# An attention and mixture-of-experts kernel: the low parts of seven batches' context made on GpSimd instead of VectorE

## The chip, the cores and the metric

The kernel runs on one core of one Trainium2 chip. The metric is the device time of the whole program in microseconds (us), as the median of three runs. The engines are TensorE (PE in the profile, with its weight loads as PEld), VectorE (DVE), ScalarE (ACT), GpSimd (POOL) and SyncE (SP), which in this kernel only issues DMAs.

## The reference

Eight batches of 512 tokens with 512 columns go through cross attention against a context of the same shape, and then through a mixture of eight experts, of which each token takes two:

```
x = x + xattn(layernorm(x), ctx, ctx, Wq, bq, Wk, bk, Wv, bv, Wo, bo)   # 16 heads of 32
x = x + ffn(layernorm(x), router, gate_up, down)                       # top 2 of 8 experts

K = ctx @ Wk.T + bk ;  V = ctx @ Wv.T + bv ;  Q = ln(x) @ Wq.T + bq
attn = softmax(Q K^T / sqrt(32)) ;  out = (attn V) @ Wo.T + bo
```

All arrays are 32 bit floats.

## The kernel before

There are three stages one after the other: attention for all batches (to about 950 us of the profile), a short routing stage, and the expert stage (39 tiles of 256 tokens). The change lies in the attention stage alone.

**Units and steps.** The attention works on 32 units. Unit u is batch b = u // 4 and a group c = u % 4 of four heads (128 columns). Step s scores and weighs unit s and meanwhile projects K, Q and V of unit s + 2. A step has eight rounds. In each round TensorE makes one pair of score tiles for the row maximum of unit s + 1 ("max", line 542), which VectorE reduces (line 802) before the next pair may be written. It also makes two score tiles of unit s (line 554), of which ScalarE takes the exponential (line 671). GpSimd adds the exponentials up into `acc` (lines 980 and 983), two heads at a time, six additions of 128x1024 to a unit. TensorE sums `acc` over the partitions (line 574) in round 3 of the next step, and the first addition of the next unit waits for that.

**Split operands.** The context is multiplied in three passes of a fast 32 bit format (`fp32r`): high by high, high by low and low by high. For this ScalarE makes the high part of the transposed context (line 637, `ctx_hi`), and the low part is the raw context less the high part (line 776, `ctx_lo`): for each batch four instructions of 128x512, one for each chunk k of 128 context columns. `ctx_raw` and `ctxT_lo` are the same memory. TensorE waits for chunk k's low part before the matmuls of that chunk (line 496), in the K projection of the first unit of a batch.

**The order of the work.** It is written out by the function `step(s)` as a list of keys by rounds. Each engine walks the same list and emits what is its own, so that an engine's program order is the order of the list, and an instruction that waits holds up all that stand behind it on its engine. The part of `step` that places the context of the next batch is the branch for c = 2:

```
elif c == 2:
    at(0, ("q", u, 0), ("ctx_hi", b + 1, 0), ("ctx_hi", b + 1, 1))
    at(1, ("q", u, 1), ("ctx_hi", b + 1, 2), ("ctx_hi", b + 1, 3), ("ctx_lo", b + 1, 0), ("ctx_lo", b + 1, 1))
    at(2, ("ctx_lo", b + 1, 2), ("ctx_lo", b + 1, 3))
    at(3, ("low", u, "q"), ("k", u, 0))
    at(4, ("k", u, 1))
```

So steps 2, 6, 10, 14, 18, 22 and 26 hold the four `ctx_lo` of one batch each, in rounds 1 and 2, and TensorE uses them in rounds 3 (chunks 0 and 1) and 4 (chunks 2 and 3). The first batch is dealt with ahead of the steps.

**What else GpSimd does in such a step**: the last addition of the unit before in round 1, two small instructions for a layer norm (lines 965 and 967), one addition of 128x512 in round 2 (line 972, the output bias), from step 11 on two indirect DMAs of the token list in round 3 (line 43), and then the additions of the step's own unit from round 4 on.

**What SP does in such a step**: it issues the DMAs that copy q and k, high and low, to the places from which the score matmuls read them (line 626), 24 issues for one unit, with loads of x (line 1062) and stores between them. The maxima of the next step's first round wait for the last of these, `ks<-k_lo`.

Of the kernel before, what the change touches and what calls it, by code (L numbers as in the profile page):

```python
# [5 lines left out]
ALU = mybir.AluOpType  # L6
ACT = mybir.ActivationFunctionType
AX = mybir.AxisListType
F32 = mybir.dt.float32
# [59 lines left out]
def attention_stage(nc, x, ctx_t, w_t, bq, bk, bv, bo, router_wt, router_b, out, xln_dram, w_rows, w_stored, token_list, listed, stored, route, ident):  # L69
# [17 lines left out]
    with ExitStack() as ctx:  # L87
# [539 lines left out]
                            source[HD * r:HD * (r + 1), :].bitcast(F32)).then_inc(landed, 16)  # L627


        def on_act(e):  # L630
            def weight_hi(n, k):
                e.wait_ge(w_in[n], 16)
# [94 lines left out]
        def on_dve(e):  # L727
# [41 lines left out]
            def weight_lo(n, k):  # L769
                e.wait_ge(w_hi_made[n].sem, w_hi_made[n][k])  # L770
                e.tensor_tensor(w[n][1][:, k, :], w_raw[n][:, k, :], w[n][0][:, k, :].bitcast(F32),
                                ALU.subtract).then_inc(w_lo_made[n].sem, 1)

            def ctx_lo(b, k):
                e.wait_ge(ctx_hi_made.sem, ctx_hi_made[b, k])
                e.tensor_tensor(ctxT[1][:, k, :], ctx_raw[:, k, :], ctxT[0][:, k, :].bitcast(F32),
                                ALU.subtract).then_inc(ctx_lo_made.sem, 1)

            def add_router_bias(n):
                e.wait_ge(logits_summed.sem, logits_summed[n])  # L780
# [129 lines left out]
            for kind, *what in ORDER:  # L910
# [12 lines left out]
                elif kind == "norm":  # L923
                    normalise(*what)
                elif kind == "x2":
                    add_residual(*what)
                elif kind == "ln2":
                    ln2(*what)
                elif kind == "turn_x" and what[0] == 0:
                    first_x_copy(what[1])  # L930
                elif kind == "stats":
                    ln1_stats(*what)
                elif kind == "mean":
                    ln1_mean(*what)
                elif kind == "shift":
                    ln1_shift(*what)
                elif kind == "split":
                    weight_lo(*what)
                elif kind == "ctx_lo":
                    ctx_lo(*what)  # L940
                elif kind == "logit_out":
                    add_router_bias(*what)
                elif kind == "best":
                    if what == [0, 0]:
                        route_consts()
                    best_experts(*what)
                elif kind == "count":
                    count_experts(*what)
                elif kind == "share":
                    share(*what)  # L950
                elif kind == "place":
                    place_tokens(*what)


        def on_pool(e):
# [48 lines left out]
            for kind, *what in ORDER:  # L1004
# [5 lines left out]
                    stack(e, "q", 0, LOW_AT["q"], lo["q"], first_lo["q"])  # L1010
                elif kind == "mean" and what[0]:
                    ln1_rstd(*what)
                elif kind == "add":
                    add_weights(*what)
                elif kind == "rstd":
# [886 lines left out]
```

## Time and profile before

| | before |
|---|---|
| median of three runs | 1720.36 us |
| the three runs | 1716.99, 1720.36, 1723.82 us |
| profiled execution, its own time | 1732.28 us |
| its span | 1730.5 us |
| attention from the first to the last maxima turned (46.8 to 926.8 us) | 880 us, 27.5 us a step |
| busy over the span: PE, DVE, ACT, POOL | 92%, 74%, 38%, 48% |

The profile is one execution, which took 12 us more than the median of the runs. A row of the timeline gives the start, the duration, the engine, the line, the operation with its output and input tiles, the count, and in brackets how long the engine sat idle before it and which instruction ended that. Rows with a count above 1 are instructions that ran back to back and are shown as one. Two neighbouring matmuls overlap, so their durations add up to more than the time they take.

### The profile page before, as it was taken

Reading aid. Unit: us, or ns where it says so; the run is one execution under the profiler, and the core shown is the slowest. Engines: PE = TensorE matmul, PEld = TensorE weight load, DVE = VectorE, ACT = ScalarE, POOL = GpSimd, SP = SyncE. Lnnn points to the kernel's source line nnn. Section 1 sums busy time; section 2 is a strip of 40 time slices with the busy share of each in tenths; the row PEclk is TensorE's granted clock in tenths of the full one; section 3 lists DMA queues with packets and bytes.
Section 4 is the critical chain, followed back from the end, with each engine's and each line's share of the span. In section 5 each row is a group of like instructions: output and inputs, shape, how many; then the busy total and the mean of one; then the engine's idle time right before and its main releaser. Section 6 shows DMA issues by size and latency. Waiting matters only on the chain. (4 is left out here: it accounts for less than half of the span.)

```text
span 1730.5 us, 30244 instructions
## 1 busy us (share of the span) xinstructions
PE 1597.8 (92%) x9612; PEld 1168.4 (68%) x9612; DVE 1272.5 (74%) x2414; ACT 658.1 (38%) x1267; POOL 837.5 (48%) x634
## 2 busy tenths in 40 slices
PE   6889999999899999999998469999999999999995
PEld 4445555555555555555553259999999998999994
DVE  5575777878668778687685668778888778777873
ACT  3354544535445445354444133223323234222320
POOL 3364656566566676566678321423333333423232
PEclk9999999999999999999999769999999999999997
DMA  6342333443434433424331161324543253324321
GB/s 221 84 121 66 106 112 85 112 104 88 121 80 111 103 94 94 116 75 110 92 99 33 56 223 50 101 85 166 172 147 123 87 204 121 107 85 149 116 86 61
DMA packets 101125, 188.99 MB, mean 109 GB/s; under 512 B 28192, under 2 KB 29600, under 8 KB 100960
## 3 DMA queue, kind: packets, MB, share of 16 engines
q1 hardware_dynamic: 79936, 124.25, 25.4%
q0 software_dynamic: 20832, 62.49, 11.4%
q8 instruction: 77, 1.26, 0.4%
q14 instruction: 88, 0.72, 0.2%
q10 hardware_dynamic: 192, 0.26, 0.0%
HBM read 204.32 MB, written 37.51 MB: 140 GB/s over the span
## 5 line engine op out<-in xcount | busy, mean ns | idle before, releaser
L802 DVE TENSOR_REDUCE negmax<-max_ps 128x2 f32<-128x1024 f32 x252 | 307.4, 1220 | 175.5 <-PE max_ps L542 174.1
L671 ACT ACTIVATE pt<-work 128x512 f32<-128x512 f32 x512 | 278.6, 595 | 263.5 <-PE work L554 256.7
L983 POOL TENSOR_TENSOR acc<-acc,pt 128x1024 f32<-128x1024 f32 x128 | 303.8, 2377 | 134.1 <-ACT pt L671 134.1
L1486 PE MATMUL gu_ps<-xgT_hi,wg_hi 128*128 128x256 f32 x1248 | 349.3, 280 | 2.3 <-DVE xgT_lo L1601 1.5
L1486 PE MATMUL gu_ps<-xgT_lo,wg_hi 128*128 128x256 f32 x1248 | 345.8, 277 | 0.0
L1486 PE MATMUL gu_ps<-xgT_hi,wg_lo 128*128 128x256 f32 x1248 | 345.5, 277 | 0.0
L980 POOL TENSOR_TENSOR acc<-pt 128x1024 f32<-128x1024 f32 x64 | 153.3, 2396 | 200.2 <-PE work L574 132.0
L1486 PEld LDWEIGHTS gu_ps<-xgT_hi,wg_hi 128*128 128x128 f32 x1248 | 235.2, 188 | 3.0 <-issue 1.9
L1747 POOL DMA_INDIRECT out<-acc,token_of x78 | 77.2, 989 | 330.4 <-DVE acc L1645 324.6
L1486 PEld LDWEIGHTS gu_ps<-xgT_lo,wg_hi 128*128 128x128 f32 x1248 | 235.5, 189 | 0.1
L1486 PEld LDWEIGHTS gu_ps<-xgT_hi,wg_lo 128*128 128x128 f32 x1248 | 235.2, 188 | 0.0
L542 PE MATMUL max_ps<-ks,qs 96*128 96x512 f32 x504 | 196.9, 472 | 29.7 <-DVE negmax L802 12.1
L1556 ACT ACTIVATE sig<-gate 128x256 f32<-128x256 f32 x156 | 65.4, 419 | 323.0 <-DVE gate L1609 321.4
L554 PE MATMUL work<-qs,ks 98*128 98x512 f32 x512 | 170.7, 411 | 12.2 <-DMA qs<-m_lo 6.6
L542 PEld LDWEIGHTS max_ps<-ks,qs 96*128 96x128 f32 x504 | 88.0, 194 | 89.8 <-issue 63.0
L566 PE MATMUL o_ps<-pt,v 128*32 128x512 f32 x1024 | 137.2, 608 | 1.6 <-ACT pt L671 1.1
L1500 PE MATMUL d_ps<-wd_hi,hid_hi 128*128 128x512 f32 x312 | 125.3, 401 | 13.7 <-DVE acc L1642 13.3
L554 PEld LDWEIGHTS work<-qs,ks 98*128 98x128 f32 x512 | 97.6, 193 | 48.9 <-issue 13.4
L1742 POOL DMA_INDIRECT acc<-out,token_of x78 | 80.7, 1035 | 101.0 <-DMA out<-acc,token_of 88.6
L504 PE MATMUL work<-xT,wq 128*128 128x512 f32 x256 | 124.0, 607 | 1.8 <-DMA wq<-wq_t 1.8
L1500 PE MATMUL d_ps<-wd_lo,hid_hi 128*128 128x512 f32 x312 | 125.0, 401 | 0.0
L1500 PE MATMUL d_ps<-wd_hi,hid_lo 128*128 128x512 f32 x312 | 124.3, 398 | 0.0
(221 smaller groups left out, 2902.2 us busy)
## 6 DMA issues: line engine op xcount, KB each, us to landing
raw_g<-w_gate_up SPq DMA_DIRECT2D x39, 2048.0 KB
raw_d<-w_down SPq DMA_DIRECT2D x39, 1024.0 KB
qs<-q_hi SPq DMA_DIRECT2D x252, 64.0 KB
ks<-k_hi SPq DMA_DIRECT2D x252, 64.0 KB
bd<-b_down SPq DMA_DIRECT2D x39, 256.0 KB
x_in<-x SPq DMA_DIRECT2D x36, 256.0 KB, 3.3
ctxT_raw<-ctx_t SPq DMA_DIRECT2D x32, 256.0 KB, 4.1
xln_dram<-x SPq DMA_DIRECT2D x32, 256.0 KB, 2.8
```

The lines of the kernel that those rows point to most:

```text
L504: ins = e.matmul(to[:, :], wq[:, k, cols], xT[:, k, :], start=(k == 0), stop=(k == C - 1))
L542: ins = e.matmul(pair_of(u, r)[:, j, :], qs[i][0:3 * HD, h, t * P:(t + 1) * P], ks[i][0:3 * HD, h, :], start=True, stop=True)
L554: e.matmul(to[:, :], ks[i][0:3 * HD + 2, h, k * P:(k + 1) * P], qs[i][0:3 * HD + 2, h, :], start=True, stop=True).then_inc(exp_ready.sem, 1)
L566: ins = e.matmul(o_ps[u % 2][HD * h:HD * (h + 1), :], v[:, k, c * P + HD * h:c * P + HD * (h + 1)], pt[k % 2][:, h, :], start=(k == 0), st ...
L671: e.activation(pt[k % 2][:, h, :], in_work("exp", u, k, h)[:, :], ACT.Exp, scale=scale).then_inc(exped.sem, 1)
L802: e.tensor_reduce(negmax[:, u % 2, n:n + 2], pair_of(u, r)[:, :, :], AX.X, ALU.max, negate=True).then_inc(maxed.sem, 1)
L980: e.tensor_tensor(acc[:, heads, :], pt[0][:, heads, :], pt[1][:, heads, :], ALU.add).then_inc(added.sem, 1)
L983: e.tensor_tensor(acc[:, heads, :], acc[:, heads, :], pt[k % 2][:, heads, :], ALU.add).then_inc(added.sem, 1)
L1486: ins = e.matmul(gu_ps[n % GU_BANKS][:, part, :], wg[s][pw][:, k, cols], xgT[s][px][:, k, :], start=(k == 0 and m == 0), stop=(k == KD - 1 ...
L1500: ins = e.matmul(d_ps[j][:, :], hid[s][px][:, k, j * P:(j + 1) * P], wd[s][pw][:, k, :], start=(k == 0 and m == 0), stop=(k == KF - 1 and ...
L1742: e.indirect_dma_start(out=acc[s][:, j, :], out_offset=None, in_=out_rows, in_offset=slot_rows(i, j)).then_inc(acc_in[s], 16)
L1747: e.indirect_dma_start(out=out_rows, out_offset=slot_rows(i, j), in_=acc[i % 2][:, j, :], in_offset=None).then_inc(scattered.sem, 16)
```

## The change

The helper that makes one low part moves out of VectorE's program and takes the engine as an argument. VectorE calls it for batch 0, GpSimd for all other batches. The waits, the semaphores, the operands and the place in the list of keys are the same.

```diff
+        def ctx_lo(e, b, k):
+            e.wait_ge(ctx_hi_made.sem, ctx_hi_made[b, k])
+            e.tensor_tensor(ctxT[1][:, k, :], ctx_raw[:, k, :], ctxT[0][:, k, :].bitcast(F32),
+                            ALU.subtract).then_inc(ctx_lo_made.sem, 1)
...
-            def ctx_lo(b, k):
-                e.wait_ge(ctx_hi_made.sem, ctx_hi_made[b, k])
-                e.tensor_tensor(ctxT[1][:, k, :], ctx_raw[:, k, :], ctxT[0][:, k, :].bitcast(F32),
-                                ALU.subtract).then_inc(ctx_lo_made.sem, 1)
...
-                elif kind == "ctx_lo":
-                    ctx_lo(*what)
+                elif kind == "ctx_lo" and what[0] == 0:
+                    ctx_lo(e, *what)
...
+                elif kind == "ctx_lo" and what[0]:
+                    ctx_lo(e, *what)
```

GpSimd's program in step 14, from the layer norm's small instructions to the unit's additions. `rstd` is the layer norm's factor, `x<-x,bo_rows` the output bias, `token_list` the indirect DMAs. Before:

```order
L965 TENSOR_TENSOR var_eps<-mv,eps_col 128x1
L967 TENSOR_TENSOR rstd<-var_eps,minus_half 128x1
L972 TENSOR_TENSOR x<-x,bo_rows 128x512
L43 DMA token_list<-consts,pos 32768x1 x2
L980 TENSOR_TENSOR acc<-pt 128x1024 x2
L983 TENSOR_TENSOR acc<-acc,pt 128x1024 x4
```

The same place in the changed kernel (line 776 is line 632 there):

```order
L965 TENSOR_TENSOR var_eps<-mv,eps_col 128x1
L967 TENSOR_TENSOR rstd<-var_eps,minus_half 128x1
L632 TENSOR_TENSOR ctxT_lo<-ctxT_raw,ctxT_hi 128x512 x2
L972 TENSOR_TENSOR x<-x,bo_rows 128x512
L632 TENSOR_TENSOR ctxT_lo<-ctxT_raw,ctxT_hi 128x512 x2
L43 DMA token_list<-consts,pos 32768x1 x2
L980 TENSOR_TENSOR acc<-pt 128x1024 x2
```

Two low parts stand ahead of the bias addition now and two behind it, and the DMAs and the unit's additions come after them.

VectorE's program in the same step, from the maxima of round 1 to the low part of q in round 3. `negmax` are the maxima, lines 899 to 908 the places of the tokens. Before:

```order
L802 TENSOR_REDUCE negmax<-max_ps 128x2
L781 TENSOR_TENSOR logits<-work,rb_rows 128x8
L776 TENSOR_TENSOR ctxT_lo<-ctxT_raw,ctxT_hi 128x512 x2
L802 TENSOR_REDUCE negmax<-max_ps 128x2
L776 TENSOR_TENSOR ctxT_lo<-ctxT_raw,ctxT_hi 128x512 x2
L802 TENSOR_REDUCE negmax<-max_ps 128x2
L899 TENSOR_TENSOR ranks<-work,consts 128x32
```

In the changed kernel:

```order
L802 TENSOR_REDUCE negmax<-max_ps 128x2
L781 TENSOR_TENSOR logits<-work,rb_rows 128x8
L802 TENSOR_REDUCE negmax<-max_ps 128x2 x2
L899 TENSOR_TENSOR ranks<-work,consts 128x32
```

The four low parts are gone from between the reductions, and nothing else on VectorE has moved. The orders of PE, ACT and SP are the same in both kernels.

## Rows read from the trace of the kernel before

**Rows 1.** The page, span and busy time of each engine.
```profile
span 1730.5 us, 30244 instructions
...
PE 1597.8 (92%) x9612; PEld 1168.4 (68%) x9612; DVE 1272.5 (74%) x2414; ACT 658.1 (38%) x1267; POOL 837.5 (48%) x634
```

**Rows 2.** Busy time in the attention's 32 steps: PE, PEld, DVE, ACT, POOL, clock, DMA.
```profile
46.80:926.80 880.00, 834.57 (x4268) 482.71 (x4269) 651.95 (x1021) 408.22 (x757) 546.45 (x322) 0.98 0.37 97
```

**Rows 3.** Groups by form, 100 to 1000 us: busy us, mean ns | idle before.
```profile
L972 POOL TENSOR_TENSOR x<-x,bo_rows 128x512 f32<-128x512 f32 x28 | 35.8, 1279 | 0.0
...
L776 DVE TENSOR_TENSOR ctxT_lo<-ctxT_raw,ctxT_hi 128x512 fp32r<-128x512 f32 x28 | 25.6, 955 | 0.0
...
L868 DVE TENSOR_TENSOR expo<-logits,best 128x32 f32<-128x32 f32 x6 | 12.0, 1998 | 0.0
```

**Rows 4.** Line 776 alone: shortest, median and longest ns.
```profile
L776 DVE TENSOR_TENSOR ctxT_lo<-ctxT_raw,ctxT_hi x32: 677/684/1806, 16.6 to 803.8; 128x512 fp32r<-128x512 f32 x32
```

**Rows 5.** The longest waits of PE in 46.8 to 926.8: total us, times, longest.
```profile
PE max_ps L542 <- DVE negmax L802: 12.1, 18, 0.9
PE max_ps L542 <- issue: 8.6, 3, 4.2
...
PE max_ps L542 <- DMA ks<-k_lo: 3.5, 1, 3.5
```

**Rows 6.** Timeline of PE in step 14 (440.8 to 469.2) and after.
```profile
450.09 0.74 PE L542 MATMUL max_ps<-ks,qs 96*128 96x512 f32 x2 [0.79 <-DVE negmax L802]
...
453.38 0.50 PE L496 MATMUL work<-ctxT_hi,wk_hi 128*128 128x512 f32 x1
...
455.81 0.40 PE L496 MATMUL work<-ctxT_hi,wk_hi 128*128 128x512 f32 x1
...
456.50 0.39 PE L496 MATMUL work<-ctxT_hi,wk_hi 128*128 128x512 f32 x1
...
473.66 1.19 PE L542 MATMUL max_ps<-ks,qs 96*128 96x512 f32 x2 [4.20 <-issue]
```

**Rows 7.** Timeline of VectorE in step 14.
```profile
446.17 2.39 DVE L776 TENSOR_TENSOR ctxT_lo<-ctxT_raw,ctxT_hi 128x512 fp32r<-128x512 f32 x2
448.81 1.22 DVE L802 TENSOR_REDUCE negmax<-max_ps 128x2 f32<-128x1024 f32 x1 [0.25 <-PE max_ps L542]
449.95 1.28 DVE L776 TENSOR_TENSOR ctxT_lo<-ctxT_raw,ctxT_hi 128x512 fp32r<-128x512 f32 x2
451.15 1.22 DVE L802 TENSOR_REDUCE negmax<-max_ps 128x2 f32<-128x1024 f32 x1
...
455.54 1.23 DVE L802 TENSOR_REDUCE negmax<-max_ps 128x2 f32<-128x1024 f32 x1 [1.30 <-PE max_ps L542]
```

**Rows 8.** Timeline of GpSimd in step 14.
```profile
446.16 1.25 POOL L972 TENSOR_TENSOR x<-x,bo_rows 128x512 f32<-128x512 f32 x1
...
449.17 0.97 POOL L43 DMA_INDIRECT token_list<-consts,pos  x1 [0.30 <-issue]
453.63 2.40 POOL L980 TENSOR_TENSOR acc<-pt 128x1024 f32<-128x1024 f32 x1 [3.49 <-PE work L574]
456.94 2.54 POOL L980 TENSOR_TENSOR acc<-pt 128x1024 f32<-128x1024 f32 x1 [0.91 <-ACT pt L671]
...
463.15 2.38 POOL L983 TENSOR_TENSOR acc<-acc,pt 128x1024 f32<-128x1024 f32 x1 [1.33 <-ACT pt L671]
```

**Rows 9.** Timeline of ScalarE in step 14.
```profile
448.93 1.14 ACT L637 ACTIVATE ctxT_hi<-ctxT_raw 128x512 fp32r<-128x512 f32 x2
...
461.99 1.09 ACT L671 ACTIVATE pt<-work 128x512 f32<-128x512 f32 x2 [1.48 <-PE work L554]
```

**Rows 10.** Timeline of SP's DMA issues in steps 14 and 18.
```profile
449.06 9.77 SPq L626 DMA_DIRECT2D qs<-q_hi  x8
...
469.60 2.41 SPq L626 DMA_DIRECT2D ks<-k_lo  x4
...
585.44 2.41 SPq L626 DMA_DIRECT2D ks<-k_lo  x4
```

## The prediction

> **What bounds the kernel now.** I read the page first, then the busy time of the attention stage, the waits of TensorE in it, and last the timelines of all five engines in one of the seven steps that the change touches. The page shows TensorE busy for 92% of the span, VectorE for 74%, GpSimd for 48% [rows 1]. In the 880 us of the attention steps TensorE is busy for 834.6 us, which leaves 45 us; VectorE is busy for 652 us, GpSimd for 546 us [rows 2]. So TensorE sets the pace, and work taken from VectorE pays only where TensorE waits for VectorE. The largest such wait is the one of the score matmuls for the row maxima, 12.1 us in 18 waits of at most 0.9 us; the other large ones wait for the copies of k and q: 3.5 us for `ks<-k_lo`, and 8.6 us in three waits for which the view names nothing ("issue") [rows 5].
>
> I take step 14 as the pattern, since the seven steps (2, 6, 10, 14, 18, 22, 26) repeat each other to a few tenths of a us around the low parts. Steps 2, 6 and 10 have no token list DMAs on GpSimd, which makes them easier, not harder.
>
> **What VectorE gives up.** Seven batches by four instructions are 28, with 955 ns in the mean, 25.6 us busy in all [rows 3]. The bare duration is the median of 684 ns; the longest is 1806 ns [rows 4]. The long one is the first of each first pair: in step 14 the pair begins at 446.17 and takes 2.39 us, while GpSimd adds the bias from 446.16 to 447.41; the second pair, with GpSimd on its DMAs, takes 1.28 us [rows 7, 8]. So a low part on VectorE now waits out an addition on GpSimd, and after the change there is nothing left to wait.
>
> How much of the 25.6 us does TensorE feel? I follow the reductions, since the score matmuls wait for these.
> - The first pair ends at 448.56. The next reduction starts at 448.81, after VectorE sat idle for 0.25 us until TensorE's scores were there [rows 7]. The pair delays nothing.
> - That reduction ends at 450.03, and the next scores start at 450.09 after a wait of 0.79 us [rows 6, 7]. This wait looks like VectorE's fault, but its reduction started as early as its scores allowed. It is the length of one reduction with too little other work for TensorE beside it, and stays.
> - The second pair ends at 451.23, so the reduction at 451.15 starts right behind it. The scores that it reads began at 450.09 and took 0.74 us, ended at 450.83, so it could start about 0.3 us sooner. The next scores were only written between the two halves of the K projection, between 453.38 and 455.81, and the reduction had ended at 452.37. There were over 2 us to spare.
> - The next reduction, at 455.54, has VectorE idle for 1.30 us ahead of it, ended by TensorE [rows 7]. There VectorE is back in step, and nothing earlier reaches past it.
>
> The gain is 0 us in each of the seven steps. The bound on the side of a gain is the whole wait of 0.79 us by seven, 5.5 us. I take 0, because the reduction ahead of the wait was itself waiting for TensorE.
>
> **What GpSimd takes on.** The trace has no subtraction to `fp32r` on GpSimd. The nearest row is the addition of the same 128x512 with two inputs, 1.28 us [rows 3]. The same elements on VectorE take 0.68 us [rows 4], the lower bound; the upper one is GpSimd's 128x1024 addition with 2.38 us [rows 8]. I take 1.28, since it has the same engine, inputs and size. 28 by 1.28 is 36 us of GpSimd, which sits idle for 334 of the 880 us [rows 2].
>
> In step 14 this comes to: GpSimd is free at 446.16. The high parts of chunks 0 and 1 were made in round 0. Low parts 0 and 1 to 448.72; the bias addition to 449.97; the high parts of chunks 2 and 3 are ready by 450.07 [rows 9]; low parts 2 and 3 to 452.6. TensorE's K projection starts at 453.38 with chunk 0, and comes to chunk 2 at 455.81 and to chunk 3 at 456.50 [rows 6]. The margins are 4.7 us for the first chunk, over 4 for chunk 2 and 3.9 for chunk 3. TensorE waits for nothing: 0 us.
>
> Queued behind them are the two token list DMAs. They now take from the end of the bias addition, 447.41, to 450.14, which is 2.73 us [rows 8], and would end at 455.3. The unit's first addition started at 453.63, after GpSimd had been idle for 3.49 us until TensorE's sums were made, so it moves back by 1.7 us, to end at 457.7. Who waits for it is the exponential of the unit's third tile, at 461.99 [rows 9]: 4.3 us of margin. The second addition starts at 457.7 instead of 456.94 and the third about 0.7 us late, and the 1.33 us of idle time ahead of the addition at 463.15 take up the rest [rows 8]. In steps 2, 6 and 10, without the DMAs, the low parts end before the first addition can start. Again 0 us.
>
> At the upper bound of 2.38 us the four would end at 448.54, 450.92, then the bias at 452.2, and 454.6 and 456.9. Chunk 3 would come 0.4 us late for 456.50, and the first addition at 462.1 would be 0.1 us late for the exponential. That is 0.5 us in a step, some 4 us in all. With the lower bound nothing changes.
>
> The row for VectorE's small operation of line 868, 128x32 in 1998 ns [rows 3], shows again that a VectorE instruction with two inputs in SBUF can wait for a whole GpSimd addition. In step 14 the token places have two such instructions (line 903), which would now start near 452.2, while the last low part runs to 452.6: 0.4 us, at most 1.28 us, against the 1.30 us of idle time that VectorE has ahead of 455.54. The cost is 0 us.
>
> The Trainium skill, in "SBUF — State Buffer", on the ports, says that GpSimd and a VectorE instruction with two inputs in SBUF share one pair of ports under an exclusive lock, so that the later one blocks for the whole of the other. The 1806 ns against 684 agree with that. By it the change takes a lock user away from VectorE and gives GpSimd a longer hold, which here would meet only line 903. The page "GPSIMD Engine Reference", section on performance against the Vector engine, speaks against the change: elementwise work with two inputs belongs on VectorE, being some two times slower on GpSimd. The trace agrees on the ratio (1279 ns to 684). If the low parts lay on the path that sets the end, that would cost 28 by 0.6 us, 17 us and not 0; by the margins above they do not.
>
> **The sum.** 0 from VectorE, 0 from GpSimd, against the profiled execution's own 1732.3 us (span 1730.5), so 1732.3. The median of the runs was 12 us below this profile, 1720.4, and I carry the difference of 0 over to it: 1720.4 us.
>
> **The rivals.**
> - Faster, by VectorE's relief. If the reduction behind the 0.79 us waits were in truth held back by the low parts, seven of these would go: 5.5 us, 1715. For more, the waits for `ks<-k_lo` and "issue" would have to go as well, 3.5 and 8.6 us [rows 5]; all of it gives 17.6 us, 1703. Against it stands that SP issues `ks<-k_lo` only at 469.60, long after VectorE made it, because SP is late with its own queue: eight issues of `qs<-q_hi` took it 9.77 us from 449.06 [rows 10]. TensorE's wait of 4.20 us to 473.66 is this wait [rows 6]. VectorE has no part in it.
> - Slower, by SP's queue. In these steps SP has little to spare: in step 18 its last `ks<-k_lo` was issued by 587.85 [rows 10], and the next scores come at about 589.5. The token list DMAs of GpSimd move from 447.6 to about 452.7, into the same time as SP's issues of q and k. If the two kinds of DMA held each other up, every one of the steps 14, 18, 22 and 26 would show the longest wait, 4.2 us, where the three "issue" waits together are 8.6 us now, 1.3 of it in a step without these DMAs. So 16.8 less 7.3 is 9.5 us, 1730. It decides from the point at which SP is 2 us later than in step 18. For it speaks that a pause of SP costs TensorE at once; against it that SP pauses in steps with and without DMAs of GpSimd beside it.
> - Slower, by a GpSimd that is slow with `fp32r`: the 4 us of the upper bound, 1724. It hardly leaves the band of no change.
>
> **How the numbers follow.** A measurement can tell about 0.5%, 8.6 us, from no change. I give the forecast of no change 0.77, GpSimd's slowness another 0.05 inside the same band, relief of VectorE 0.08 and SP's queue 0.10. Relief has its small form of 5.5 us inside the band and its large form outside; of the 0.08 I put 0.02 inside. SP's queue has 0.01 inside. So faster 0.06, same 0.85, slower 0.09. The range starts from the runs' own spread of 3.4 us to each side, and takes in the gain of 5.5 us below and the 4 us above with a part of SP's case: 1713 to 1728.
>
> **What would show it right or wrong.** Right: on GpSimd 28 rows of line 632 of about 1.28 us; VectorE's busy time lower by some 26 us, GpSimd's higher by 36; the 0.79 us wait ahead of the scores in each of the seven steps still there; no wait of the K projection for GpSimd; the unit's first addition 1.7 us later in step 14 with no exponential waiting for it. Wrong: a row of line 496 that waits for `ctxT_lo`, low parts much over 1.3 us, exponentials that wait for GpSimd, the 0.79 us waits gone, or waits for `ks<-k_lo` longer or more frequent in the step behind each step with c = 2.

## The result and the profile after

| | before | after |
|---|---|---|
| median of the runs made side by side | 1722.09 us (1716.99 to 1723.84, 4 runs) | 1739.62 us (1734.64 to 1741.89, 4 runs) |
| profiled execution, its own time | 1732.28 us | 1740.52 us |
| its span | 1730.5 us | 1738.8 us |
| attention, first to last maxima turned | 879.9 us | 887.8 us |

The change makes the kernel slower: after to before is 1.0103, 95% interval 1.007 to 1.0135, some 17.5 us. A second measurement of the same kernel gave 1.0111 (1.0088 to 1.0134). The forecast was no change, 1720.4 us, with a range of 1713 to 1728 us.

The page of the kernel after, span and busy time, as in [rows 1]:

```profile
span 1738.8 us, 30244 instructions
...
PE 1598.9 (92%) x9612; PEld 1168.4 (67%) x9612; DVE 1265.2 (73%) x2386; ACT 656.4 (38%) x1267; POOL 867.7 (50%) x662
```

The line view of the new low part in the kernel after (shortest, median and longest ns; first and last start):

```profile
L632 POOL TENSOR_TENSOR ctxT_lo<-ctxT_raw,ctxT_hi x28: 1251/1269/1285, 107.9 to 807.4; 128x512 fp32r<-128x512 f32 x28
L632 DVE TENSOR_TENSOR ctxT_lo<-ctxT_raw,ctxT_hi x4: 681/681/683, 16.9 to 20.5; 128x512 fp32r<-128x512 f32 x4
```

So the 28 low parts cost GpSimd 1.27 us each, as forecast; its busy time rose by 30.2 us. But VectorE, which lost 28 instructions of 25.6 us [rows 3], is only 7.3 us less busy. Some instructions on VectorE must have grown instead. The one that matters is found in the waits of TensorE from the first to the last step of the kernel after (total us, times, longest), which is [rows 5] again:

```profile
PE max_ps L542 <- DVE negmax L802: 12.7, 20, 0.8
PE work L459 <- DVE x L771: 9.2, 3, 3.1
...
PE max_ps L542 <- issue: 4.0, 3, 2.1
...
PE max_ps L542 <- DMA ks<-k_lo: 3.1, 1, 3.1
```

The second line is new: in the kernel before, line 459 waits for no layer norm. Line 459 turns the layer norm's result over, and line 771 (766 in the kernel before) makes it: `x = (x - mean) * rstd`, one input tile in SBUF and two factors a row. Its line view, after and then before:

```profile
L771 DVE TENSOR_SCALAR x<-x,mv,rstd x28: 536/538/5524, 196.3 to 966.4; 128x512 f32<-128x512 f32 x28
```

```profile
L766 DVE TENSOR_SCALAR x<-x,mv,rstd x28: 536/539/1496, 194.7 to 958.8; 128x512 f32<-128x512 f32 x28
```

The median is the same, the longest went from 1.5 to 5.5 us. Three instructions take 5.5 us, one in each of the steps 18, 22 and 26. GpSimd in step 18 of the kernel after:

```profile
566.90 2.49 POOL L632 TENSOR_TENSOR ctxT_lo<-ctxT_raw,ctxT_hi 128x512 fp32r<-128x512 f32 x2
569.35 1.27 POOL L972 TENSOR_TENSOR x<-x,bo_rows 128x512 f32<-128x512 f32 x1
570.59 2.51 POOL L632 TENSOR_TENSOR ctxT_lo<-ctxT_raw,ctxT_hi 128x512 fp32r<-128x512 f32 x2
573.27 1.04 POOL L43 DMA_INDIRECT token_list<-consts,pos  x1 [0.18 <-issue]
574.62 0.96 POOL L43 DMA_INDIRECT token_list<-consts,pos  x1 [0.30 <-issue]
575.61 4.74 POOL L980 TENSOR_TENSOR acc<-pt 128x1024 f32<-128x1024 f32 x2
580.32 2.33 POOL L983 TENSOR_TENSOR acc<-acc,pt 128x1024 f32<-128x1024 f32 x1
```

VectorE in the same stretch:

```profile
573.86 0.43 DVE L908 CAST pos<-pos_f 128x8 int32<-128x8 f32 x1
...
576.27 1.23 DVE L802 TENSOR_REDUCE negmax<-max_ps 128x2 f32<-128x1024 f32 x1 [1.58 <-PE max_ps L542]
577.41 5.52 DVE L771 TENSOR_SCALAR x<-x,mv,rstd 128x512 f32<-128x512 f32 x1
582.86 0.94 DVE L819 RECIPROCAL inv<-inv 128x128 f32<-128x128 f32 x1
```

And VectorE and GpSimd at that place in the kernel before:

```profile
576.70 0.54 DVE L766 TENSOR_SCALAR x<-x,mv,rstd 128x512 f32<-128x512 f32 x1
```

```profile
573.64 2.41 POOL L980 TENSOR_TENSOR acc<-pt 128x1024 f32<-128x1024 f32 x1 [3.49 <-PE work L574]
576.96 2.52 POOL L980 TENSOR_TENSOR acc<-pt 128x1024 f32<-128x1024 f32 x1 [0.91 <-ACT pt L671]
```

Read with the step's start (561.56 after, 560.84 before), the layer norm comes 15.86 us into the step in both kernels. Before, the first addition ran from 12.80 to 15.20 and the second from 16.12: the layer norm started in the gap of 0.9 us between them, and it was the second addition that took 2.52 us instead of 2.4. After, the first addition starts at 14.05, since the two list DMAs end only then. It now ends later than the second could have started, so the first three additions run without a gap, from 575.61 to 582.65, and the layer norm is done at 582.93. It waited not for the one addition that ran when it came, but for the whole row of three.

Not every instruction of VectorE waits so. The reciprocal of line 819 reads and writes SBUF alone, too, and 38 of its 124 instances began while a GpSimd operation of over 1 us was running, but none took longer than 0.95 us:

```profile
L819 DVE RECIPROCAL inv<-inv x124: 939/942/952, 93.0 to 950.0; 128x128 f32<-128x128 f32 x124
```

TensorE in the kernel after, step 18:

```profile
578.95 1.06 PE L566 MATMUL o_ps<-pt,v 128*32 128x512 f32 x8
583.08 1.08 PE L459 MATMUL work<-ident,x 128*128 128x128 f32 x4 [3.07 <-DVE x L771]
583.82 0.56 PE L518 MATMUL work<-wv_hi,ctxT_hi 128*128 128x256 f32 x1
584.18 0.41 PE L518 MATMUL work<-wv_lo,ctxT_hi 128*128 128x256 f32 x1
...
586.19 0.28 PE L518 MATMUL work<-wv_hi,ctxT_lo 128*128 128x256 f32 x1
```

Busy time by stretches of that step in the kernel after (PE, PEld, DVE, ACT, POOL, granted clock, DMA share, GB/s):

```profile
566.00:582.00 16.00, 13.22 (x67) 6.64 (x66) 10.87 (x13) 8.27 (x15) 15.41 (x13) 1.00 0.53 59
583.00:586.00 3.00, 2.92 (x14) 2.95 (x15) 2.90 (x4) 0.60 (x1) 0.00 (x0) 0.50 0.59 146
586.00:592.00 6.00, 6.00 (x36) 3.85 (x35) 4.59 (x8) 1.69 (x4) 2.38 (x1) 1.00 0.81 232
```

TensorE stood for 3.07 us, and then the granted clock was 0.50 (1.2 GHz) for the next 3 us, in which the matmuls of line 518 start 0.21 us apart instead of 0.115. The step takes 32.99 us instead of 28.38; 3.07 of the 4.6 us are the pause, and the lower clock makes up the rest. Three such steps are 13.8 us.

Step 14 of the same profile escaped. Its first two additions and its layer norm:

```profile
458.50 4.96 POOL L980 TENSOR_TENSOR acc<-pt 128x1024 f32<-128x1024 f32 x2
```

```profile
460.57 0.64 DVE L771 TENSOR_SCALAR x<-x,mv,rstd 128x512 f32<-128x512 f32 x1
```

Here the layer norm came 0.3 us later, 16.14 us into the step, and so did the exponentials that the second addition reads: they were ready 0.16 us before the first addition ended, against 0.45 us in step 18. The pair takes 4.96 us instead of 4.74, and the layer norm got in between the two. Which of the two delays let it in is not shown.

### The profile page after: what moved, and what is told of

Same layout as the page of the kernel before. It is cut to its first block and busy times, and to the rows that moved or that the text cites. A ratio compares the mean times of both kernels' runs of the same rounds, so it can differ in the third digit from the quotient of the medians.

```text
span 1738.8 us, 30244 instructions
## 1 busy us (share of the span) xinstructions
PE 1598.9 (92%) x9612; PEld 1168.4 (67%) x9612; DVE 1265.2 (73%) x2386; ACT 656.4 (38%) x1267; POOL 867.7 (50%) x662
## 3 DMA queue, kind: packets, MB, share of 16 engines
q0 software_dynamic: 20832, 62.49, 11.1%
## 5 line engine op out<-in xcount | busy, mean ns | idle before, releaser
L542 PE MATMUL max_ps<-ks,qs 96*128 96x512 f32 x504 | 195.8, 470 | 26.4 <-DVE negmax L802 12.7
L554 PE MATMUL work<-qs,ks 98*128 98x512 f32 x512 | 169.6, 409 | 11.6 <-DMA qs<-m_lo 6.7
L1502 PE MATMUL d_ps<-wd_hi,hid_hi 128*128 128x512 f32 x312 | 125.7, 403 | 14.5 <-DVE acc L1644 13.2
```

The lines of the kernel that those rows point to most:

```text
L542: ins = e.matmul(pair_of(u, r)[:, j, :], qs[i][0:3 * HD, h, t * P:(t + 1) * P], ks[i][0:3 * HD, h, :], start=True, stop=True)
L554: e.matmul(to[:, :], ks[i][0:3 * HD + 2, h, k * P:(k + 1) * P], qs[i][0:3 * HD + 2, h, :], start=True, stop=True).then_inc(exp_ready.sem, 1)
L1502: ins = e.matmul(d_ps[j][:, :], hid[s][px][:, k, j * P:(j + 1) * P], wd[s][pw][:, k, :], start=(k == 0 and m == 0), stop=(k == KF - 1 and ...
```

## The experiments

**The theories.** A: the first addition comes so late that GpSimd's gap closes, and the layer norm of line 771 waits inside its own duration until GpSimd pauses. The main rival, D in most of the expectations: the token list DMAs of GpSimd, moved to a later time, meet SP's copies of q and k, and the next step's scores wait for these. Further rivals say in the expectations themselves what they are.

I cut each profile into steps by the starts of line 548, and count for the last four steps with c = 2 (14, 18, 22, 26) what they take over 28.36 us each, and for the steps behind them (c = 3: 15, 19, 23, 27) what they take over 26.97. In the latter the excess is mostly TensorE waiting for the copies of k and q, and its lower clock behind such a wait; in the three versions with the lists moved out of the c = 2 steps it is something else, as told below for lists_out_after. A ratio is taken against runs of the kernel before on the same chip, whose medians were 1722.1 to 1725.4 us, so times of different versions compare best by their ratios.

| kernel | ratio to before (95%) | c = 2 steps over, us | c = 3 steps over, us |
|---|---|---|---|
| before | 1 | 1.2 | 13.3 |
| after | 1.0103 (1.007, 1.0135) | 14.2 | 4.3 |
| after_again | 1.0111 (1.0088, 1.0134) | 15.7 | 7.1 |
| first_three | 1.0005 (0.9985, 1.0025) | 0.3 | 7.2 |
| last_four | 1.0079 (1.0054, 1.0104) | 19.7 | 0.1 |
| ln2_accum | 1.0048 (1.003, 1.0067) | 0.2 | 7.6 |
| dummy_pool | 1.0110 (1.0071, 1.0149) | 25.8 | 0.0 |
| half | 1.0017 (1.0001, 1.0032) | 0.2 | 12.7 |
| lists_later | 1.0136 (1.0109, 1.0162) | 1.3 | 23.6 |
| ln2_sooner | 1.0089 (1.0062, 1.0116) | 0.1 | 20.0 |
| lists_out_after | 1.0021 (1.0, 1.0042) | 0.4 | 12.4 |
| lists_out_before | 1.0027 (1.001, 1.0045) | 0.6 | 11.4 |
| x_later | 0.9955 (0.9934, 0.9975) | 0.4 | 8.0 |
| both | 0.9998 (0.9979, 1.0017) | 1.4 | 11.1 |
| filler2 | 1.0045 (1.0024, 1.0065) | 13.5 | 1.1 |
| filler4 | 1.0054 (1.003, 1.0077) | 16.6 | 3.5 |
| bias_later | 1.0040 (1.0023, 1.0057) | 11.6 | 0.3 |
| x_later_lists | 0.9994 (0.9972, 1.0016) | 9.8 | 0.0 |

The two columns are of one execution each, the ratio of several. The profile of before is an unlucky one: its own time is 10 us over the 1722.09 us, and its c = 3 column is higher than that of first_three, which is as fast as before.

**The changed kernel again.** after_again is the changed kernel with no edit, for its time beside other runs.

> The changed kernel once more, for a second profile of it. Theory A: 1739 to 1740; each of the steps 14, 18, 22 and 26 either takes 28.4 to 28.7 us or some 33.0, according to whether line 771 got in between the two additions, with at least three of the four at 33.0.

It gave 1742.57 us and the same picture: line 771 with 5.50 to 5.52 us in steps 18, 22 and 26, 0.66 in step 14.

**Which batches.** first_three moves only the low parts of batches 1 to 3 to GpSimd (steps 2, 6 and 10, which hold no list DMAs), last_four only those of batches 4 to 7 (steps 14 to 26).

```diff
-                elif kind == "ctx_lo" and what[0]:
+                elif kind == "ctx_lo" and 0 < what[0] < 4:     # first_three
+                elif kind == "ctx_lo" and what[0] > 3:         # last_four
```

VectorE makes the others.

> The low parts of batches 1 to 3 on GpSimd (steps 2, 6, 10), all others on VectorE as before. Theory A, the port: in the changed kernel the list DMAs and the unit's first two additions on GpSimd move back by some 1.5 us, GpSimd then runs additions back to back, and VectorE's layer norm instruction (line 771, 5.5 us instead of 0.54 in steps 18, 22 and 26) waits for them. In steps 2, 6 and 10 there are no list DMAs, the first addition isn't late, so the time is that of before, 1722 (within 2 us), and line 771 never takes over 1.5 us. Theory B, a cost in proportion to the low parts moved: 3/7 of 17.5 us, 1729.6.

> The low parts of batches 4 to 7 on GpSimd (steps 14, 18, 22, 26), all others on VectorE. Theory A: the whole loss, 1739 to 1740, with three or four of these steps 4.6 us longer (28.4 to 33.0). Theory B: 4/7 of 17.5 us, 1732.1.

first_three took 1722.58 us, as expected. last_four took 1735.46 us, which is some 13.6 us by the ratio and a little less than the whole loss. Line 771 in the profile of last_four:

```profile
L771 DVE TENSOR_SCALAR x<-x,mv,rstd x28: 536/540/5495, 195.8 to 964.2; 128x512 f32<-128x512 f32 x28
```

The cost lies in the steps that hold the list DMAs. In last_four all four of them have the long layer norm (5.47 to 5.50 us).

**Taking the stall away at its own instruction.** ln2_accum is the changed kernel with one more output for line 771, a sum over the row. Its `x` is then not the layer norm's, so the text reads only its times.

```diff
-                                ALU.subtract, ALU.mult).then_inc(ln2_made.sem, 1)
+                                ALU.subtract, ALU.mult, accum_out=unused[:, :]).then_inc(ln2_made.sem, 1)
```

> The changed kernel, with VectorE's layer norm instruction (tensor_scalar, 128x512 from SBUF to SBUF) in the form that also writes an accumulator to a tile that nobody reads. The Trainium skill, SBUF - State Buffer, section Who interferes with whom, has this form leave GpSimd's ports alone. Theory A with that rule: the instruction takes longer on its own (some 0.7 us instead of 0.54, the 128x512 rows of one element a cycle) but never 5.5 us, no transposition (line 459) waits 3 us for it, and the time is near that of before: 1722 to 1725. If what it waits for isn't the ports, it still takes 5.5 us in three or four steps and the time is 1740.

Line 772 (771 in the changed kernel) in its profile:

```profile
L772 DVE TENSOR_SCALAR_CACHE_REDUCE x<-x,mv,rstd x28: 795/797/805, 198.9 to 958.2; 128x512 f32<-128x512 f32 x28
```

It takes 0.80 us instead of 0.54, but never more than 0.81, though GpSimd's first additions are as late and as close as in the changed kernel (14.03 us into step 18, 4.77 us for two). So the instruction did as expected, and the c = 2 steps have no excess. The time did not: 1730.06 us is over the 1722 to 1725 expected. The stall is gone and some 9 of the 17.5 us with it; 8.2 us stay (5 to 11.5 by the interval), which the stall does not explain. They can't be laid on the low parts either. Beside first_three, the profile of ln2_accum is 9.9 us longer, 1.3 us of it between the first and last maxima turned and 7.6 us in the stages behind the attention, which the change does not touch and which here work on other values. That part of the span lies between 796.9 and 804.5 us in all profiles, 803.8 in that of before.

**Making the stall without the change.** dummy_pool is the kernel before, with one extra GpSimd operation of 128x512 wherever the change puts a low part on GpSimd.

```diff
+                elif kind == "ctx_lo" and what[0]:
+                    extra()      # bo_rows = bo_rows * 1, on GpSimd
```

> The kernel before, where VectorE makes all low parts, with four additional instructions of 128x512 on GpSimd at the places where the changed kernel has its low parts (the bias row times one, in place, which changes no value). Theory A: GpSimd's later additions are the cause, whoever makes the low parts, so the time is that of the changed kernel or more, about 1740, with line 766 at 3 to 5.5 us in steps 14, 18, 22 and 26. Theory C, the loss comes from what VectorE no longer does or from TensorE's wait for GpSimd's low parts: 1722.

TensorE's waits in its profile from 440 us on:

```profile
PE work L459 <- DVE x L766: 16.2, 4, 4.1
```

It took 1742.45 us, as expected. Line 766 takes 6.5 us in all four steps and TensorE stands for 4.04. So who makes the low parts does not matter to the stall; that GpSimd is late does.

**Half of the change.** half moves only chunks 0 and 1 to GpSimd, which fits into its idle time ahead of the first addition.

```diff
-                elif kind == "ctx_lo" and what[0]:
+                elif kind == "ctx_lo" and what[0] and what[1] < 2:
```

> The changed kernel with only chunks 0 and 1 of batches 1 to 7 on GpSimd, chunks 2 and 3 back on VectorE. Theory A: GpSimd is free some 2.5 us sooner, before the sums are made, so the first addition isn't late, and all 17.5 us come back: 1722. Theory B, in proportion: half the loss, 1731.

(The low parts of each engine have a semaphore of their own here.) The first addition is back at 12.8 to 13.0, line 771 at 0.54 us in these steps, and the time, 1727.57 us, within 0.2% of before.

**Making room by moving the list DMAs or the layer norm.** lists_later issues the list DMAs of the c = 2 steps in round 7; ln2_sooner makes the layer norm a round earlier, with the store of its result, which SP issues.

```diff
-                at(3, ("list", g, t))
+                at(7 if c == 2 else 3, ("list", g, t))                            # lists_later
-                at(2 if s == B * C else 4 if c == 2 else 3, ("ln2", s - 5))
+                at(2 if s == B * C else 3, ("ln2", s - 5))                        # ln2_sooner
```

> The changed kernel, with GpSimd's two token list DMAs of each step with c = 2 moved from round 3 to round 7, behind the unit's third addition. All 28 low parts stay on GpSimd. Theory A, the port: the unit's first two additions are on time again (first at 12.8 us into the step, second at 16.1, a gap between them), line 771 takes 0.54 us, the steps with c = 2 take 28.4 us and not 33.0, and the time is that of before: 1722. Theory B, that low parts on GpSimd cost by themselves: 1739.

> The changed kernel, with the layer norm of the steps with c = 2 (line 771 on VectorE, and its store on SP) in round 3, as in the other steps, instead of round 4. GpSimd's program and its late additions are as in the changed kernel. Theory A: line 771 then stands beside the last low part or the list DMAs of GpSimd, waits at most 1.3 us for one instruction, and no transposition waits for it; the steps 18, 22 and 26 take 28.4 us and not 33.0, the time is 1722 to 1727. If late additions cost by another way (ScalarE, the sums), it stays at 1740.

Both removed the stall (line 771 at 0.54 and at most 0.63 us in the c = 2 steps, which take what they took before), and both missed the 1722 to 1727 us expected, with 1745.72 and 1741.74: they lost more in the c = 3 steps, 23.6 and 20.0 us, than the stall costs. TensorE's waits from 440 us on, first of lists_later, then ln2_sooner, then the kernel before:

```profile
PE max_ps L542 <- issue: 15.5, 3, 7.3
```

```profile
PE max_ps L542 <- issue: 12.5, 3, 6.7
```

```profile
PE max_ps L542 <- issue: 7.3, 2, 4.2
```

These are the first scores of a c = 3 step, which wait for `ks<-k_lo`. Where TensorE waits for it in a step without list DMAs, they come 1.6 us after SP's last issue of it. In lists_later it was 7.9, 8.6 and 3.7 us, in ln2_sooner up to 8.1 us: the issue is on time and the data is late. In other steps SP itself pauses, as in [rows 10]. So the place of the list DMAs among SP's copies seems to have a price of its own. It is not the place alone: ln2_sooner has the lists where the changed kernel has them, and there the same scores come 3.9 us (5.5 in after_again) after the last issue in step 15. Below the stall the lateness is hidden: a TensorE that is 4.6 us late for another reason does not wait for these copies, which is why the c = 3 column of last_four and dummy_pool is nearly 0.

**The list DMAs out of these steps.** lists_out_after and lists_out_before move them into the next step, for the changed kernel and the kernel before alike.

```diff
-            if g in groups[:-3]:
+            if g in groups[:-3] and (c != 2 or s + 2 not in units):
+            if c == 3 and s - 15 in range(0, 16, T):
+                at(3, ("list", (s - 15) // T, 3))
```

> The changed kernel, with the two token list DMAs of the steps 14, 18, 22 and 26 moved to round 3 of the step behind each, which has no low parts (steps 15, 19, 23 and 27 then have four). Theory A, the port, says that the loss goes: line 771 at 0.54 us in all steps, steps with c = 2 at 28.4 us. And theory D, formed from the traces so far, says that GpSimd's token list DMAs slow the DMA queues: where they stand at 7 to 9 us into a step, SP's eight issues of q's high part took 7.4 to 9.8 us in most of the steps 14, 22 and 26 instead of 5.0; where they stood at 25 to 28 us, k's low part landed up to 8.6 us after its last issue instead of 1.6, and TensorE waited up to 7.3 us. With them out of these steps, D expects waits of at most 1 us at the start of the steps 15, 19, 23 and 27, so 1716 to 1719, under the kernel before. Without D: 1722 to 1725.

> The same move of the token list DMAs in the kernel before, with all low parts on VectorE. Theory D: the same time as lists_out_after, 1716 to 1719, since without the collision it is of no account which engine makes the low parts. If GpSimd's low parts cost or gain something by themselves, the two differ by over 3 us.

This is the plainest comparison of the two engines: with nothing that makes GpSimd late, the low parts on GpSimd give 1730.46 us and on VectorE 1729.53. The difference of 0.9 us for 28 instructions is within the noise, the 0 of the forecast. The 1716 to 1719 us expected for both failed to come. Their c = 3 steps are as long as before for another reason: in step 15 of lists_out_after TensorE waits 3.55 us for ScalarE's copy of the turned layer norm, in step 19 2.77 us for a reduction. That the four list DMAs in these steps are behind these waits is likely and not shown.

**SP's queue.** x_later is the kernel before with three of the four loads of x behind the copies of k and q; both joins it with lists_out_before.

```diff
-                for t in range(T):
-                    at(1 + t, ("load_x", b + 2, t))
+                at(1, ("load_x", b + 2, 0))
+                at(6, ("load_x", b + 2, 1))
...
+                at(0, ("load_x", b + 2, 2))
+                at(1, ("load_x", b + 2, 3))
```

> The kernel before, with three of the four loads of x that SP issues among the copies of q and k in a step with c = 2 moved behind them (round 6, and rounds 0 and 1 of the next step). Theory A says that TensorE's waits of 1.3 to 4.2 us at the start of the steps with c = 3 are SP's lateness alone: SP's last issue of k's low part then comes 1.7 us sooner, and up to 1.7 us of each such wait goes, some 4 to 6 us in all: 1717. If SP's lateness were made up of something else (its pauses between issues), no change: 1722.

> The kernel before with both moves: the loads of x behind the copies of q and k (x_later), and the token list DMAs of the steps with c = 2 in the step behind (lists_out_before). x_later alone was 6 us under the kernel before, lists_out_before is expected some 4 us under it, mostly from the same waits: 1713 to 1717, the fastest of all. If the two save the same waits, no better than x_later, 1718.

In five of the seven steps behind one with c = 2 SP issues the last `ks<-k_lo` 1.0 to 1.7 us sooner than in the profile of before, and x_later takes 1718.71 us (1717 was expected), by the ratio 7.7 us less than before and the fastest of all. Joined with the moved lists the gain is gone, against the 1713 to 1717 us expected.

**The stall with no DMA moved.** filler2 and filler4 are the kernel before with 2 or 4 extra GpSimd operations in the steps 14, 18, 22 and 26, behind the list DMAs.

```diff
+                    if t == 3 and g < 4:
+                        for _ in range(2):     # filler4: 4
+                            extra()
```

> The kernel before (low parts on VectorE) with 2 extra GpSimd operations of one 128x512 bias row times one in steps 14, 18, 22 and 26, behind the list DMAs and ahead of the unit's first addition; no DMA is moved. Theory A (the first addition must not come so late that it runs into the next one while the layer norm's tensor_scalar stands between them): GpSimd is through with the extra work at about 12.3 us into the step, the first addition still starts at 12.8, line 766 stays at 0.54 us, steps at 28.4, time 1722 to 1725. Rival B (any GpSimd work added in these steps costs, by its port or by its heat): about 4 us, a quarter of the changed kernel's loss or more, 1727 or above.

> The same with 4 such operations: GpSimd is through at about 15.3 us, so that the first addition starts 2.5 us late and joins the second; still no DMA is moved. Theory A: line 766 takes 5.5 us or more in all four steps, TensorE stands 3 to 4 us ahead of the transposes, steps of 33 to 35 us, 1738 to 1746. Rival C (the changed kernel's loss is that of the later list DMAs): steps keep 28.4 to 29, time below 1728.

Theory A's numbers missed both. filler2 should have been free and cost 1.0045, the time that rival B had; filler4 should have cost 1738 to 1746 and took 1734.64, more than rival C allowed. GpSimd in step 18 of filler2 (it starts at 559.04):

```profile
568.37 2.51 POOL L980 TENSOR_TENSOR bo_rows<-bo_rows,ones 128x512 f32<-128x512 f32 x2
571.86 2.39 POOL L990 TENSOR_TENSOR acc<-pt 128x1024 f32<-128x1024 f32 x1 [0.98 <-PE work L574]
576.45 2.38 POOL L990 TENSOR_TENSOR acc<-pt 128x1024 f32<-128x1024 f32 x1 [2.19 <-ACT pt L671]
579.19 2.38 POOL L993 TENSOR_TENSOR acc<-acc,pt 128x1024 f32<-128x1024 f32 x1 [0.35 <-ACT pt L671]
```

VectorE beside it:

```profile
568.17 3.26 DVE L776 TENSOR_TENSOR ctxT_lo<-ctxT_raw,ctxT_hi 128x512 fp32r<-128x512 f32 x2
571.35 1.21 DVE L802 TENSOR_REDUCE negmax<-max_ps 128x2 f32<-128x1024 f32 x1
...
572.70 1.83 DVE L903 TENSOR_TENSOR hot<-hot,ranks 128x32 f32<-128x32 f32 x2
...
576.88 2.24 DVE L766 TENSOR_SCALAR x<-x,mv,rstd 128x512 f32<-128x512 f32 x1
```

The first addition is on time, as expected. But the two fillers hold up VectorE's second low part (3.26 us for the pair instead of 1.28), the reduction and the token places behind it come 2 us late, and so they run into the first addition, which they had passed by a hair: in the kernel before the last of them, line 908, was done at 12.7 us into the step and the addition started at 12.8. They wait until it ends at 574.25, TensorE's next tile waits 1.28 us for line 908, and the step takes 31.73 us. The stall is the same, at another instruction.

That wait also makes the second addition late, and the layer norm, coming at 576.88, meets it: it takes 2.24 us. It is done 0.29 us after the addition's end at 578.83, in the gap of 0.35 us in which GpSimd waits for an exponential before its third addition. No transposition waits for it, but VectorE is late behind it, and TensorE later waits 0.72 us for the low part of k. So a gap of 0.35 us is enough to let VectorE in. In filler4 the additions begin at 14.5, 1.7 us late and not the 2.5 expected, and the conversion of line 908 waits for the first one: TensorE stands for 2.0 to 2.1 us in three of the steps and for 1.3 in the fourth, the layer norm takes 2.2 us, and the steps take 32.5 us.

**Both causes undone at once.** bias_later is the changed kernel with the list DMAs ahead of the low parts and the bias addition moved to round 6.

```diff
-                at(2, ("bo", s - 2))
+                at(6 if c == 2 and s + 2 in units else 2, ("bo", s - 2))
-                at(3, ("list", g, t))
+                at(1 if c == 2 and s + 2 in units else 3, ("list", g, t))
```

> The changed kernel, all 28 units with the low parts on GpSimd, but in the steps with c = 2 the list DMAs are issued in round 1 ahead of the low parts and the bias addition (line 972) moves to round 6, into GpSimd's gap. Theory A+D (port stall, and list DMAs not later than before): the first addition at 13.0 us or sooner, line 771 at 0.54 us, steps 28.4, no late k copies, 1722 within 3. Rival: the low parts cost something by themselves on GpSimd (slower by more than 4 us with both undone). If the bias addition in the gap pushes the first addition behind 13.5 us, the stall is back and the time is near 1740.

It missed too: 1731.25 us, 1.0040, over the 1722 within 3 us that were expected. In step 18 the first addition is at 12.80 and the c = 3 steps are clean (0.3 us over), but GpSimd in step 18 (from 557.13) reads:

```profile
564.98 4.98 POOL L632 TENSOR_TENSOR ctxT_lo<-ctxT_raw,ctxT_hi 128x512 fp32r<-128x512 f32 x4
569.93 2.39 POOL L980 TENSOR_TENSOR acc<-pt 128x1024 f32<-128x1024 f32 x1
```

And VectorE:

```profile
568.31 0.18 DVE L899 TENSOR_TENSOR ranks<-work,consts 128x32 f32<-128x32 f32 x1
568.52 3.85 DVE L903 TENSOR_TENSOR hot<-hot,ranks 128x32 f32<-128x32 f32 x2
```

Two instructions of 128x32, 0.42 us elsewhere, take 3.85 us: the first came at 568.52, while the low parts ran until 569.96, and the second was let in at the end of the addition, 572.32. There was no gap between the low parts and the addition. In steps 14 and 22 it is the conversion of line 908 that waits for the addition, and in all four the layer norm takes 2.2 us, as in filler2. The steps take 31.0 to 31.5 us.

**The lists sooner in the fastest version.**

```diff
-                at(3, ("list", g, t))
+                at(1 if c == 2 and s + 2 in units else 3, ("list", g, t))   # on x_later
```

> The kernel before with three of the four x loads moved behind the k and q copies (as x_later, 0.9955) and the list DMAs of the steps with c = 2 in round 1, ahead of the bias addition. Theory D: the lists are served before SP issues the next unit's copies, SP's pauses shrink, and it is 0.994 to 0.9955 of before. If the lists in round 1 meet other copies, 0.9955 to 1.0.

The c = 3 steps have no excess left at all, which shows what the place of the list DMAs is worth. But the bias addition behind them runs into VectorE's low parts, and line 910 (908 in the others) comes just too late for the gap:

```profile
565.92 2.38 DVE L910 CAST pos<-pos_f 128x8 int32<-128x8 f32 x1
```

The first addition began at 565.88. A conversion of eight columns, 0.17 us in x_later, waits for it, the layer norm behind it takes 2.2 us, and the c = 2 steps take 30.8 us. What the one side gave, the other took: 0.9994, where 0.994 to 0.9955 was expected.

## Why the prediction was wrong

**The step that failed** is the sentence "Again 0 us" on what is queued behind the low parts. I asked who waits for the additions of GpSimd, found the exponential with 4.3 us of margin, and stopped. The right question is also who runs beside them. With a first addition 1.7 us later I had it end at 457.7 and the second start there: my own numbers said that the gap between the two closes. I did not look at what stood in it, line 766 on VectorE.

**The lock was named and given to the wrong instruction.** The prediction drew on the Trainium skill, "SBUF — State Buffer", for instructions with two inputs in SBUF, and checked line 903. The Trainium skill, same page, section "Who interferes with whom", also lists the plain scalar operation (except in the form that writes an accumulator) and the cast among the ones that can take the shared ports. The trace agrees: 5.52 us for line 771 and 2.38 us for the cast of line 910 beside an addition, and never over 0.81 us in the accumulator form.

**And its price was taken too low.** I put the most that one collision can cost at 1.28 us, one GpSimd instruction. The Trainium skill, in the same section, says that whoever issues first has the shared ports for the whole instruction and the other blocks. The trace shows more than that: VectorE waited for all that GpSimd ran without a gap, three additions in step 18 (until 582.65, having come at 577.41), low parts and an addition in bias_later. A gap of 0.35 us was enough in filler2.

**The smaller terms.** VectorE's gain of 0 was right: the wait of 0.79 us ahead of the scores (0.85 in steps 2 and 6, as before) is there in all seven steps of the kernel after. The low part's 1.28 us was right (1.27). TensorE waits for no low part. The first addition came 1.25 us late instead of 1.7.

**The rival of SP's queue** was priced at 9.5 us. In the kernel after it is not seen at that price: its c = 3 steps lost 4.3 us (7.1 in after_again), where before lost 13.3 and first_three, as fast as before, 7.2. Its form was wrong, too: SP's eight issues of `qs<-q_hi` took 9.8, 5.0, 8.3 and 7.9 us in the steps 14, 18, 22 and 26 before and at most 5.9 after; it is the data that arrives later. That the place of the list DMAs matters shows in the other versions: bias_later and x_later_lists, with these DMAs early, have c = 3 steps with no excess, lists_later has 23.6 us. The two costs do not add up. Each c = 2 step with the stall takes 4.6 us more, four of them 18.5 us, and 13.6 of these are measured in last_four; the difference fits the lateness of copies that the stall covers, since the c = 3 column falls from 7.2 us in first_three to 0.1.

**The sum.** Between the two profiles the c = 2 steps give 13.0 us, the c = 3 steps give back 9.0, and the other steps add 3.9, which makes the attention's 7.9 us. The profile of before had an unusual share of late copies and was 10 us over its runs' median. I carried "0" over from that profile to the median. The difference that was measured, 17.5 us (12 to 23 by the interval), is more than the 13.8 us of three stalled steps, and in both profiles of the changed kernel step 14 escaped. The stall explains most of it; the other 4 us or so are not accounted for.

**What stays open.** How an indirect DMA of GpSimd delays copies that SP has already issued was not shown, nor that it alone does: only that the delay changes with when they are issued. ln2_accum is 8.2 us slower than before although the attention in its profile shows no more excess than that of first_three, which is not slower. The profiles are single executions, and this I can't resolve. Why step 14 runs 0.3 us late in both profiles of the changed kernel, and not in that of last_four, is open as well.

## What to carry to other kernels

When an engine's work is moved in time, ask who runs beside it and not only who waits for it. Here three kinds of VectorE instructions in SBUF waited until GpSimd had a gap: the scalar operation with one input (line 771), those with two inputs (lines 776 and 903) and a conversion of eight columns (line 908); reciprocals and the accumulator form did not. Where such an instruction stands in a gap of GpSimd and TensorE needs its result soon, that gap belongs to the critical path, and a change that closes it can cost TensorE a whole row of GpSimd's work and some time at the lower clock after that. The wait is inside the instruction's own duration, so look for instructions that grew. Costs that cover each other in a step have to be removed together, and the kernel that came out best here, by 0.45%, did not touch the arithmetic: it took three loads out of the way of a DMA queue.

## What the runs showed of the hardware

- VectorE's wait ran over instruction borders of GpSimd as long as these were back to back: 5.5 us (three additions, the first of them three quarters over), 6.5 us in dummy_pool, 3.85 us for two instructions in bias_later.
- Of VectorE's instructions within SBUF, the 124 reciprocals of line 819 took 0.94 to 0.95 us, beside a GpSimd operation or not.
- The form of line 771 that also sums over the row costs 0.80 us instead of 0.54, and did not wait beside the same additions.
- GpSimd's 128x512 with two inputs takes 1.27 us whether the output is `fp32r` or not.
- A pause of TensorE of 3.07 us was followed by 3 us at a granted clock of 0.50. Of the 4.6 us that such a step loses, 1.5 us, what the pause leaves over, is an estimate of this. In filler2, with a pause of 1.28 us, the clock stayed at 1.00.
- Scores that wait for the last `k_lo` start 1.6 us after SP's issue of its copy in steps without list DMAs, and up to 8.6 us after it in lists_later, where these were issued late in the step.
